# Scan stage of a two-block model: the second half of the values is convolved by VectorE instead of TensorE

## What is computed

```python
zxbcdt = jnp.einsum('bld,ed->ble', u, in_proj_w)
z, xBC, dt = jnp.split(zxbcdt, [D_INNER, D_INNER + CONV_DIM], axis=-1)
conv = conv_general_dilated(transpose(xBC), conv_w[:, None, :], window_strides=(1,),
                            padding=[(D_CONV - 1, 0)], feature_group_count=CONV_DIM)
xBC = silu(transpose(conv) + conv_b)
x, Bm, Cm = jnp.split(xBC, [D_INNER, D_INNER + D_STATE], axis=-1)
dt = softplus(dt + dt_bias); dA = exp(dt * A)
# for each token: h = h * dA + dt * B x ;  y = h C ;  then y + D * x, times silu(z)
```

## Time and profile before

| | |
|---|---|
| runs | 1815.37, 1801.58, 1801.46 us |
| the profiled execution, its time | 1806.22 us |
| its span in the trace | 1804.4 us |
| TensorE busy, whole span | 1671.3 us (93%) |
| VectorE busy, whole span | 1272.1 us (70%) |
| ScalarE busy, whole span | 1192.6 us (66%) |
| scan stage in the trace | 1406.3 to 1529.2 us |

### The profile page before, as it was taken

One profiled execution on the slowest core, in us unless ns is written; L12 is line 12 of the kernel. 1 busy time (PEld: TensorE's weight loads), 2 busy tenths in 40 slices (PEclk: granted clock), 3 DMA queues, 4 the chain that ended last, 5 costly groups with the idle time before them and its releaser, 6 DMA issues. The chain is left out here.

```text
span 1804.4 us, 25875 instructions
## 1 busy us (share of the span) xinstructions
PE 1671.3 (93%) x9970; PEld 785.9 (44%) x9970; DVE 1272.1 (70%) x1818; ACT 1192.6 (66%) x2434; POOL 199.1 (11%) x187
## 2 busy tenths in 40 slices
PE   6999999999999999869999999999887788699997
PEld 3433333333333333245444444455565455344443
DVE  4888888888888888168788678675476566255555
ACT  4578888888788888845677777777536664333432
POOL 1100000000000000041001000111245000000100
PEclk9899999999999999989899999999978899699999
DMA  1000000000000000010000000000100000202220
GB/s 62 1 1 1 1 1 1 1 1 1 1 1 1 1 1 1 1 47 1 1 1 1 1 1 1 1 2 1 37 1 1 12 1 28 122 20 94 100 90 21
DMA packets 7274, 29.98 MB, mean 17 GB/s; under 512 B 680, under 2 KB 2736, under 8 KB 4848
## 3 DMA queue, kind: packets, MB, share of 16 engines
q1 hardware_dynamic: 7152, 28.33, 4.2%
HBM read 27.15 MB, written 1.18 MB: 16 GB/s over the span
## 5 line engine op out<-in xcount | busy, mean ns | idle before, releaser
L910 DVE TENSOR_REDUCE a_part_max<-a_ps 128x2 f32<-128x1024 f32 x512 | 602.9, 1221 | 90.6 <-PE a_ps L713 90.0
L895 ACT ACTIVATE a_probs<-a_ps 128x512 f32<-128x512 f32 x1024 | 532.9, 615 | 130.7 <-PE a_ps L808 128.5
L910 DVE TENSOR_REDUCE f_part_max<-f_ps 128x2 f32<-128x1024 f32 (+3 forms) x320 | 328.3, 1062 | 126.9 <-PE f_ps L713 66.4
L808 PE MATMUL a_ps<-a_q_shift,a_KA 64*128 64x512 f32 x1024 | 367.1, 446 | 4.0 <-POOL a_q_shift L692 2.7
L895 ACT ACTIVATE f_probs<-f_ps 128x512 f32<-128x512 f32 (+3 forms) x640 | 300.4, 538 | 102.2 <-PE f_ps L808 49.5
L808 PEld LDWEIGHTS a_ps<-a_q_shift,a_KA 64*128 64x128 f32 x1024 | 166.2, 186 | 290.4 <-ACT a_probs L895 275.2
L713 PE MATMUL a_ps<-a_KA,a_q_open 64*128 64x512 f32 x1024 | 276.1, 466 | 4.9 <-DVE a_part_max L910 4.2
L828 PE MATMUL a_psO<-a_probs,a_VA 128*32 128x512 f32 x2048 | 274.6, 608 | 3.9 <-ACT a_probs L895 3.9
L808 PE MATMUL f_ps<-f_q_shift,f_KA 64*128 64x512 f32 (+3 forms) x640 | 223.8, 436 | 5.5 <-POOL f_q_shift L692 2.5
L713 PE MATMUL f_ps<-f_KA,f_q_open 64*128 64x512 f32 (+3 forms) x640 | 169.0, 428 | 7.3 <-DVE f_part_max L910 6.1
L808 PEld LDWEIGHTS f_ps<-f_q_shift,f_KA 64*128 64x128 f32 x640 | 106.1, 188 | 150.2 <-ACT f_probs L895 138.7
(11 more groups left out here) (343 smaller groups left out, 1776.7 us busy)
## 6 DMA issues: line engine op xcount, KB each, us to landing
t_c_all<-c_rows SPq DMA_DIRECT2D x16, 1024.0 KB, 7.6
experts_w<-in_experts SPq DMA_DIRECT2D x1, 3264.0 KB, 12.0
W<-in_weights SPq DMA_DIRECT2D x1, 1574.0 KB, 6.4
out<-X SPq DMA_DIRECT2D x4, 256.0 KB, 6.6
K<-in_consts SPq DMA_DIRECT2D x1, 644.0 KB, 7.0
R<-in_rows SPq DMA_DIRECT2D x1, 530.0 KB, 6.0
W<-in_weights SPq DMA_DIRECT2D x1, 512.0 KB, 6.8
mx_conv_rows<-in_conv_rows SPq DMA_DIRECT2D x1, 512.0 KB, 3.3
```

The lines of the kernel that those rows point to most:

```text
L808: mm = pe.matmul(bank(r)[:, lo:512], g.KA[rows, 2 * n + jp, P * s:P * s + P], q_shift[rows, u % 2, jp, lo:512], start=True, stop=not diag)
L895: nc.scalar.activation(probs[:, st % 2, j, lo:512], bank(r)[:, lo:512], ACT.Exp, scale=SCALE).then_inc(ring_read, 1)
L910: dve.tensor_reduce(part_max[:, 4 * q + 2 * jp:4 * q + 2 * jp + 2, c], ps1[:, k % 2, :, 0:b - a], AX_X, ALU.max).then_inc(max_read, 1)
```

## The change

The first half of x is still convolved by TensorE; the second half joins B and C. The items of a block become `COPY_X, COPY_B, COPY_C, X0, T_X0, Z0, T_X1, Z1, T_B`, `pad` has three rows, VectorE convolves three rows per block (the third at the third chunk), and ScalarE copies three banks. On ScalarE `silu_taps` of the values comes before `skips(n, 0)`, those of B and C after `silu_z(n, 0)`. The core of the diff:

```diff
-    ITEMS, COPY_B, COPY_C, X0, X1, T_X0, Z0, T_X1, Z1, T_B = 9, 0, 1, 2, 3, 4, 5, 6, 7, 8
+    ITEMS, COPY_X, COPY_B, COPY_C, X0, T_X0, Z0, T_X1, Z1, T_B = 9, 0, 1, 2, 3, 4, 5, 6, 7, 8
...
-        pad = sb("pad", [P, 2, CONV - 1 + S])
+        pad = sb("pad", [P, 3, CONV - 1 + S])
...
+                project(0, COPY_X)
                 project(0, COPY_B)
                 project(0, COPY_C)
                 decays_of(0)
-                convolve(0, 0)
-                convolve(0, 1)
+                convolve(0)
                 turn_x(0, 0)
...
                         if n < NB and i == 0:
+                            project(n, COPY_X)
                             project(n, COPY_B)
+                        if n < NB and i == 1:
                             project(n, COPY_C)
-                        if n < NB and i == 1:
-                            convolve(n, 0)
+                            convolve(n)
                         if n < NB and i == 2:
-                            convolve(n, 1)
                             turn_x(n, 0)
...
                 def silu_taps(n, x):
 
-                    act.wait_ge(conv_done, 2 * n + x + 1)
-                    nc.scalar.activation(xbc[:, n % 2, 2 + x, :], xbc[:, n % 2, 2 + x, :], ACT.Silu).then_inc(silu_bc, 1)
+                    act.wait_ge(conv_done, 3 * n + x + 1)
+                    nc.scalar.activation(xbc[:, n % 2, 1 + x, :], xbc[:, n % 2, 1 + x, :], ACT.Silu)\
+                       .then_inc(silu_bc if x else silu_x, 1)
...
-                    copy_pad(n, 0)
-                    copy_pad(n, 1)
+                    for x in range(3):
+                        copy_pad(n, x)
                     for c in range(4 * n, 4 * n + 4):
                         spread_a(c)
...
-                    silu_conv(n, 0)
-                    silu_conv(n, 1)
+                    silu_conv(n)
                     silu_taps(n, 0)
-                    silu_taps(n, 1)
                     skips(n, 0)
                     silu_z(n, 0)
+                    silu_taps(n, 1)
+                    silu_taps(n, 2)
                     skips(n, 1)
                     silu_z(n, 1)
...
-                convolve(0, 0)
-                convolve(0, 1)
+                for x in range(3):
+                    convolve(0, x)
...
-                        if n < NB and i < 2:
+                        if n < NB and i < 3:
                             convolve(n, i)
```

More of the change, by code:

```diff
@@ L1603, in project, with convolve @@
                 def project(n, item):
-                    at = 2 + item
+                    at = 1 + item
                     pe.matmul(slot(n, item), g.w("mxbc")[:, P * at:P * at + P], g.UT[:, U0 + 512 * n:U0 + 512 * n + 512],
                               start=True, stop=True).then_inc(ring_ps, 1)
-                def convolve(n, x):
-                    bank = slot(n, X0 + x)
-                    if n == 0 and x == 0:
+                def convolve(n):
+                    bank = slot(n, X0)
+                    if n == 0:
                         pe.wait_ge(taps_in, 1)
                     for k in range(CONV):
-                        mm = pe.matmul(bank, taps[:, k, P * x:P * x + P], g.UT[:, 512 * n + k:512 * n + k + 512],
+                        mm = pe.matmul(bank, taps[:, k, 0:P], g.UT[:, 512 * n + k:512 * n + k + 512],
                                        start=(k == 0), stop=(k == CONV - 1))
@@ L1733, in copy_pad, with silu_conv @@
                     nc.scalar.copy(pad[:, x, U0 + 512 * n:U0 + 512 * n + 512], ring(ITEMS * n + x)).then_inc(ring_read, 1)
-                def silu_conv(n, x):
-                    k = ITEMS * n + X0 + x
+                def silu_conv(n):
+                    k = ITEMS * n + X0
                     act.wait_ge(ring_ps, k + 1)
-                    nc.scalar.activation(xbc[:, n % 2, x, :], ring(k), ACT.Silu, bias=g.c("mconvb", x)).then_inc(silu_x, 1)
-                    act.wait_ge(silu_x, 2 * n + x + 1)
+                    nc.scalar.activation(xbc[:, n % 2, 0, :], ring(k), ACT.Silu, bias=g.c("mconvb", 0)).then_inc(silu_x, 1)
+                    act.wait_ge(silu_x, 2 * n + 1)
                     act.nop().then_inc(ring_read, 1)
                 def silu_taps(n, x):
-                    act.wait_ge(conv_done, 2 * n + x + 1)
-                    nc.scalar.activation(xbc[:, n % 2, 2 + x, :], xbc[:, n % 2, 2 + x, :], ACT.Silu).then_inc(silu_bc, 1)
+                    act.wait_ge(conv_done, 3 * n + x + 1)
+                    nc.scalar.activation(xbc[:, n % 2, 1 + x, :], xbc[:, n % 2, 1 + x, :], ACT.Silu)\
+                       .then_inc(silu_bc if x else silu_x, 1)
                 def skips(n, x):
@@ L1798, in _ @@
                 copy_pad(0, 1)
+                copy_pad(0, 2)
                 exponent(0)
@@ L1801, in _ @@
                 spread_a(2)
[L1802 to L1805, removed]
+                silu_conv(0)
+                for x in range(3):
+                    silu_taps(0, x)
                 skips(0, 0)
@@ L1842, in convolve @@
                 def convolve(n, x):
-                    out = xbc[:, n % 2, 2 + x, :]
+                    out = xbc[:, n % 2, 1 + x, :]
                     tap = lambda k: pad[:, x, 512 * n + k:512 * n + k + 512]
@@ L1849, in convolve @@
                         dve.wait_ge(y_ps, 4 * (n - 2) + 4)
-                    at = conv.up(dve.tensor_scalar(out, tap(CONV - 1), g.c("mconv", CONV * (2 + x) + CONV - 1),
-                                                   g.c("mconvb", 2 + x), ALU.mult, ALU.add))
+                    at = conv.up(dve.tensor_scalar(out, tap(CONV - 1), g.c("mconv", CONV * (1 + x) + CONV - 1),
+                                                   g.c("mconvb", 1 + x), ALU.mult, ALU.add))
                     for k in range(CONV - 1):
                         dve.wait_ge(conv_step, at)
-                        ins = dve.scalar_tensor_tensor(out=out, in0=tap(k), scalar=g.c("mconv", CONV * (2 + x) + k),
+                        ins = dve.scalar_tensor_tensor(out=out, in0=tap(k), scalar=g.c("mconv", CONV * (1 + x) + k),
                                                        in1=out, op0=ALU.mult, op1=ALU.add)
```

## The result

The changed kernel takes 1817.1 us (median of 18 runs) where before takes 1806.0 us (18 runs): 11.2 us between the medians. The ratio over all runs is 1.0068, 95% interval 1.0052 to 1.0084, which is 12.3 us more (9.4 to 15.2). The stage is compared from its first product to the first product of the stage behind it, cut at the weighings of chunks 0, 4, 8 and 12: the prologue, the blocks b = 0, 1 and 2, and the last block.

The account below looks back on a forecast made before the run. VectorE's list up to the first values was taken to bound each block. Waits of +7.7 us and clock falls of +7.4 gave +15.1 on 1801.58, 1816.7 us, stated as 1816.5, range 1806 to 1823.

Parts of the forecast that it names:

- What bounds the block: Each block is set by VectorE's list up to the first values, which ends 0.8 us after TensorE's.
- Part 1: TensorE in the blocks: removed products save 2.58 us a block, 10.3 in four, worth nothing on the path.
- Part 2: VectorE ahead of values(n, 0): the third convolution adds 2.82, 2.45 and 2.82 us in blocks 0 to 2, +8.1 in sum.
- Part 3: ScalarE: later third copy and silus add 0.1 us each in blocks 1 and 2; a 2 us turn_x wait stays hidden.
- Part 4: Prologue: the third convolution hides in VectorE's idle time and turn_x(0, 1) starts earlier, -0.6 us (-1.5 to +0.5).
- Part 5: TensorE's new pauses in blocks 0 to 2 halve the clock: 2.0, 2.7 and 2.7 us, +7.4 (0 to 12).
- The signs named: Block 2 29.8 us without or 32 to 33 with a clock fall; VectorE's stretch 19.1, later idle at least 6.4.
- One sign of being wrong: Prediction wrong if values(n, 0) comes less than 2.4 us later in its block.
- Rival A: The clock holds in the stage, so only the first four parts count: +7.7 us, 1809.3 us; chance 0.2.
- Rival B: Slow clock loses 4 us in each block and TensorE's list ends later in the next: +19.7 us, 1821; chance 0.12.
- Rival C: TensorE's list, not VectorE's, sets the block, gaining all 10.3 us: 1791.3 us; chance 0.06 with its half-way version.

Follow-up runs that it names:

- relief alone: Kernel before with one tap product instead of four for x's second half, VectorE's list unchanged: stage 123.96 us against 123.15, ratio 1.0014.
- VectorE's work alone: Kernel before plus a third VectorE convolution into a row nobody reads, TensorE keeping both halves: stage 134.20 us, ratio 1.0053 to before.
- third convolution late: Changed kernel with blocks 1 to 3's third convolution moved behind values(n, 1) and its silu behind copy_b: stage 125.95 us, ratio 1.0015 to before.
- filled kernel: Changed kernel plus products nobody reads in TensorE's pauses ahead of the transposes (also "the pauses filled"): stage 131.89 us, ratio 1.0038 to before.
- rearranged kernels: Projections, copies and convolutions moved into the block before, values earlier: changed kernel 0.9918 and 0.9943 of before, kernel before 0.9965; changed with filled prologue 0.9933.

## Why the prediction was right, point by point

Forecast were 1816.5 us and +15.1 us; measured 1817.1 us and +12.3 us. The sign and the steps hold, and one term, the clock's, is too large. That the two absolute times agree within 0.6 us is luck: the forecast started from 1801.6 us, the median of three runs, and before took 1806.0 us in the 18 runs of the comparison. This is 4.4 us more and made up for the term that was too large.

- **What bounds the block.** Right. VectorE's list up to `values(n, 0)` went from 16.27 to 19.09 us in block 2, forecast 19.1. The relief alone left block 2 at 26.89 us, VectorE's work alone gave the whole loss.
- **Part 1, the removed products**: worth nothing on the path in block 2, as forecast. In block 1 of the relief alone 0.47 us came back, and VectorE's 0.37 us of idle time is gone there; with the third convolution in place nothing comes back in any block (20.85 us up to the transposes with the relief, 20.87 without). In the prologue the relief alone gained 1.54 us.
- **Part 2, the third convolution**, forecast +2.82, +2.45 and +2.82 us. Up to the transposes the changed kernel shows +2.81, +2.33 and +2.82. In block 0 the chain moved as described (TensorE idle for 6.87 us, forecast 6.9).
- **Part 3, ScalarE**: forecast as +0.2 us; in sum it cannot be seen. The new wait at `turn_x(n, 0)`, forecast as 2 us, was 1.60 us in block 2 and hidden.
- **Part 4, the prologue**: -0.6 forecast, -0.17 and -0.34 measured. `turn_x(0, 1)` did come 0.95 us earlier in the stage, but the clock fell at about 1430.6 behind a pause of 2.20 us, which the step had not counted. Nor had it counted that the tap products wait for GpSimd: they began 0.58 us later in the stage than before.
- **Part 5, the clock**: the mechanism was right, the size was off. The term was +7.4 us for three falls, 2.0, 2.7 and 2.7. Behind the transposes the first profile shows 2.02, 1.82 and 1.43, together 5.3 us; the second shows 2.15, 0 and 0.77, together 2.9. So block 0 was sized rightly, and blocks 1 and 2 too large. The step took their loss from a stretch of full work, 5.3 us at half speed, and let pauses stretch it. But 0.7 us of the slow work only took the place of TensorE's wait at `turn_b`, and the fall of block 1 in the second profile came so early that it was over while VectorE's list was still running. In block 0 the transposes behind the pauses of 3.68, 4.09, 4.30 and 6.87 us (twice) all took 1.09 us, that is, they ran at the slow clock.
- **The signs named.** Block 2 took 29.70 us without a fall (forecast 29.8), but 31.14 and 30.47 with one, not 32 to 33: this is the size of part 5 again. VectorE's idle time ahead of the weighing of chunk 12 was 7.34 and 6.76 us (at least 6.4). TensorE's busy time fell by 2.3 us in each of blocks 1 and 2 where the clock held, in the kernel with the third convolution late. One sign of being wrong came true by a hair: `values(n, 0)` of block 1 came 2.34 us later (19.24 us after the weighing against 16.90), where less than 2.4 was to count against the prediction. The limit had been set 0.05 us under the step's own 2.45. The mechanism is not touched, as VectorE's work alone gives the same 19.25.
- **Rival A** (+7.7 us, the clock holds) is what the filled kernel shows in blocks 1 and 2; in time it had 1.0038, +6.9 us. **Rival B** did not come: the parts up to the transposes show no TensorE list that ends later. **Rival C**, the rule of the busiest engine, fails in this order. The Trainium skill (Perfetto Trace Analysis, section Identifying the Most-Contended Engine) names the engine with the highest occupancy as the one to optimize first, but has TensorE judged by other measures than its matmul time, one of them the share of its weight loads. In the earlier trace rows these are busy 69.2 of 124 us, less than VectorE's 82.1, so what failed is the prediction's reading of the page by matmul time; this reading comes out only in the rearranged kernels, where TensorE is busy 23.5 of 24.1 us. The Trainium skill (TensorE: Matmul & The Clock Gate, section HAM oscillation — how this bites in real kernels) says that a long pause of TensorE in each turn of a loop can bring the clock down in every turn. Both profiles of the changed kernel agree, with a fall in each of the three blocks, one of them behind a pause of only 1.77 us; in VectorE's work alone the clock held through block 1, with a pause of 3.12 us.

## What to carry to other kernels

Before work is moved from the busiest engine, look at which list ends last at each point where the engines meet: here an engine busy for two thirds of the stage set the block, because its load stood ahead of the meeting point and its idle time behind it. The same offload lengthened the stage by 10.5 to 13.1 us ahead of that point and shortened it by 5.3 to 8.5 us once the receiving list had been emptied there. Relief of TensorE that turns into a pause can cost more than it gives, as the clock falls; look at the granted clock behind each new pause.

## What had not been expected of the hardware

The length of a pause did not decide alone whether the clock fell. TensorE's last pause in the prologue is 2.13 or 2.14 us long in nine profiles, ahead of the same product; its middle before stands in the earlier trace rows. The clock stayed at 1.00 behind it in four profiles (before, the first of the changed kernel, VectorE's work alone, the third convolution late) and fell in five (the pauses filled, the relief alone, three of the rearranged kernels). In the blocks it fell once behind 1.77 us, in the changed kernel's second profile, and held once behind 3.12 us, in VectorE's work alone. Behind all nine pauses of 3.62 to 6.87 us it was down. The first row is the stretch behind the 2.13 us with the pauses filled, then come the pauses of 1.77 and 3.12 us, whose transposes took 1.08 and 0.66 us:

```profile
1428.00:1433.00 5.00, 5.00 (x20) 3.22 (x18) 2.82 (x6) 1.77 (x3) 0.00 (x0) 0.72 0.00 0
...
1479.84 1.08 PE L1633 MATMUL mx_ps<-K,mx_xbc 128*128 128x128 f32 x4 [1.77 <-ACTq L1741]
...
1488.58 0.66 PE L1634 MATMUL mx_ps<-K,mx_xbc 128*128 128x128 f32 x4 [3.12 <-ACT mx_skip L1758]
```

In the changed kernel's prologue a pause of 2.20 us, after another of 0.98 us, brought 0.52:

```profile
1430.90:1434.10 3.20, 3.20 (x12) 2.35 (x11) 1.92 (x2) 1.44 (x3) 0.00 (x0) 0.52 0.00 0
```

What decides between 1.77 and 3.12 us stays open. And a clock once down can stay down under full work. In the second attention block, whose code the change does not touch, before had 1.00 and the changed kernel's first profile 0.50 in the same stretch, TensorE busy throughout in both, with 151 matmul records against 86. First before, then the changed kernel:

```profile
813.00:843.60 30.60, 30.17 (x151) 16.91 (x150) 23.73 (x23) 19.03 (x30) 4.88 (x5) 1.00 0.01 1
```

```profile
813.00:843.60 30.60, 30.36 (x86) 15.77 (x86) 15.56 (x14) 11.82 (x18) 1.20 (x1) 0.50 0.00 1
```

The scan began at 1402.3 to 1416.8 us in the profiles of this study, though nothing ahead of it differed. This long slow stretch goes with the late starts: it stands in the three profiles whose scan began at 1415.7 to 1416.8 us (mean clock from 814 to 1280 us 0.96) and in none of the eight that began at 1402.3 to 1407.5 us (0.99). This is why the stages are compared here, and why the whole time needs many runs. What keeps the clock down there stays open.
